# A graph network on one core: the attention row terms through memory, a reordered opening, and a bias added by DMA

## The reference

```python
h = relu(layernorm(x)); skip = x
for l in range(3):
    si, sj = h @ attn_w[l, :d], h @ attn_w[l, d:]
    scores = leaky(si[:, :, None] + sj[:, None, :] + attn_b[l], 0.2)
    attn = softmax(where(adj + eye > 0, scores, -inf))
    a = layernorm(h + einsum('bij,bjd->bid', attn, h), g1[l], beta1[l])
    h = layernorm(a + gelu(a @ W1[l] + b1[l]) @ W2[l] + b2[l], g2[l], beta2[l])
return skip + h
```

## Time and profile before

| what | value |
|---|---|
| median of 3 runs | 2274.11 us (2273.81 to 2275.63) |
| the profiled execution, its own time | 2274.6 us |
| span of its instructions | 2272.8 us |
| mean granted TensorE clock | 0.996 |
| longest waits of PE | DVE s_j 20.9 us (2 times), DVE g_lo 19.5 us (24 times) |
| longest gaps in the trace of PE before slot 1 | 13.1 us before the first transposes, 7.8, 6.6, 5.2 and 5.0 us |

### The profile page before, as it was taken

The page is one execution under the profiler, slowest core; times in us unless marked ns, Lnnn a source line. Parts: engine busy times, 40 slices in busy tenths (PEclk is TensorE's granted clock), DMA queues, the critical chain, the costliest instruction groups (busy, mean ns, idle before and its releaser), DMA issues.

```text
span 2272.8 us, 46153 instructions
## 1 busy us (share of the span) xinstructions
PE 2202.7 (97%) x15456; PEld 1520.7 (67%) x15456; DVE 1869.1 (82%) x5889; ACT 1887.6 (83%) x3496; POOL 1908.4 (84%) x1640
## 2 busy tenths in 40 slices
...
DMA packets 383722, 145.23 MB, mean 64 GB/s; under 512 B 314240, under 2 KB 381824, under 8 KB 383488
## 3 DMA queue, kind: packets, MB, share of 16 engines
...
...
## 4 chain that ended last, share of the span: by engine, by line
PE 79%; DVE 17%; issue 3%; ACT 1%; DMA 1%; POOL 0%; DVEq 0%; SPq 0%
PE p_hid L448 36%; PE p_pair L462 35%; PE p_pair L500 5%; DVE g_lo L682 3%; DVE bn L689 3%; DVE res L765 2%; DVE adj_in L710 2%; DVE dots L727 2%; PE p_pair L486 2%; DVE dots L730 1%; DVE p_lo L777 1%; DVE mv L694 0%; PE p_pair L473 0%; DMA pT_hi<-p_hi 0%; DMA adj_in<-in_adj 0%
## 5 line engine op out<-in xcount | busy, mean ns | idle before, releaser
L462 PE MATMUL p_pair<-w_hi,g_hi 128*128 128x256 f16 x3072 | 839.1, 273 | 0.0
L462 PE MATMUL p_pair<-w_lo,g_hi 128*128 128x256 f16 x3072 | 839.1, 273 | 0.0
L462 PE MATMUL p_pair<-w_hi,g_lo 128*128 128x256 f16 x3072 | 839.0, 273 | 0.0
L556 ACT ACTIVATE p_hid<-p_hid,b_eff 128x512 f32<-128x512 f32 x768 | 503.4, 655 | 293.3 <-PE p_hid L448 291.8
L682 DVE TENSOR_TENSOR g_lo<-p_hid,g_hi 128x512 f16<-128x512 f32 x768 | 518.0, 683 | 44.0 <-ACT g_hi L561 36.1
L448 PE MATMUL p_hid<-hT_hi,w_hi 128*128 128x512 f16 x1536 | 458.2, 380 | 26.0 <-DVE g_lo L682 19.5
L561 ACT ACTIVATE g_hi<-p_hid 128x512 f16<-128x512 f32 x768 | 458.7, 597 | 24.3
L448 PE MATMUL p_hid<-hT_lo,w_hi 128*128 128x512 f16 x1536 | 458.6, 380 | 0.9 <-DMA hT_lo<-h_lo 0.9
L448 PE MATMUL p_hid<-hT_hi,w_lo 128*128 128x512 f16 x1536 | 457.8, 380 | 0.0
L937 POOL TENSOR_TENSOR rstd<-var_eps,minus_half 128x4 f32<-128x4 f32 x224 | 230.5, 1029 | 266.1 <-DVE minus_mean L697 266.1
L462 PEld LDWEIGHTS p_pair<-w_hi,g_hi 128*128 128x128 f16 x3072 | 301.2, 98 | 107.6 <-issue 0.8
...
## 6 DMA issues: line engine op xcount, KB each, us to landing
...
adj_in<-in_adj SPq DMA_DIRECT2D x32, 256.0 KB, 3.3
...
pT_hi<-p_hi SPq DMA_TRANSPOSE x96, 2.4
pT_lo<-p_lo SPq DMA_TRANSPOSE x96, 2.4
hT_hi<-h_hi SPq DMA_TRANSPOSE x96, 3.6
```

The costliest lines, as they stand in the source:

```text
L462: mm = pe.matmul(ff_banks(s)[:, t, :], g[i][:, nodes], w[l][:, c, :], start=(c == 0 and t % 2 == 0 and n == 0), stop=(c == C - 1 and n == ...
L556: act.activation(p_hid[k][:], p_hid[k][:], ACT.Gelu, bias=b1_eff[:, l, c:c + 1], scale=1.0 / WSCALE).then_inc(gelu_ready, 1)
```

## The change

It has four parts.

- **Row terms.** From item 4 on, `spread_sj` is gone from PE. SP writes the 512 numbers s_j (128 nodes by 4 graphs, four bytes each) of item s+4 to a buffer in memory at the head of slot s, and at the end of the slot reads them back as one row broadcast to all partitions, 256 KB, into one SBUF buffer `sj_rows`. `add_scores` reads that buffer.
- **One slot further ahead.** Dot products, input statistics, normalization and input load run one slot earlier than before. The mask stays at s+4.
- **Opening.** The probabilities of items 0 and 1 are transposed by PE into PSUM; ACT copies the high half, DVE subtracts for the low half. Loads, statistics, residuals and deviations are reordered; inputs 4 to 7 of the first round are loaded straight into their feature buffers, masks 4 and 5 are made by POOL in slots 0 and 1. Pieces of the weights of layers 1 and 2 move from slots 0 to 3 to slots 3 to 11, one in each slot and engine; the bias folds move to slots 2 and 7. Slots 0 to 11 are written out, and the loop body is slots 12 to 35.
- **b2** is added to the rows of beta1 by an accumulating DMA of POOL.

The changed lines, with the engine's block above each part; counters and names that only follow from them are left out:

```diff
-FIRST_LOOP_SLOT = 4
+FIRST_LOOP_SLOT = 12
...
-FOLD_AT = {4: 1, 6: 2}
+FOLD_AT = {5: 1, 10: 2}
...
+sj_rows = sb("sj_rows", [P, T, N])
+sj_memory = [nc.dram_tensor(f"sj_memory{i}", [T, N], F32).ap() for i in range(2)]
...
+def pair_half(i, h):
+    return p_pair[i][:, 2 * h:2 * h + 2, :].rearrange("p a (u n) -> p (a u) n", n=N)
 def sj_bank(s):
-    return p_pair[s % 2][:, 0:2, :].rearrange("p a (u n) -> p (a u) n", n=N)
+    return pair_half(1, 1) if s == 2 else pair_half(s % 2, 0)
+def by_memory(r, s):
+    return not (isinstance(r, int) and r == 0 and s < 4)
+def sj_total(r, s):
+    return total(r, s, 16, 16 - 4 * 16)
+def bias_bank(s):
+    return pair_half(s % 2, 0)
+def first_pT(i):
+    return pair_half(0, 1 - i)
...
-act_pieces = dict(zip([(0, 6), (0, 7), (1, 0), (1, 3), (2, 0), (2, 3), (3, 0), (3, 3)], pieces[4:]))
-dve_pieces = dict(zip([(0, 7), (1, 1), (1, 4), (2, 1), (2, 4), (2, 7), (3, 1), (3, 4)], pieces[4:]))
+act_pieces = dict(zip([(3, 0), (4, 3), (5, 3), (6, 3), (7, 3), (8, 3), (9, 3), (10, 3)], pieces[4:]))
+dve_pieces = dict(zip([(s, 0) for s in range(4, 12)], pieces[4:]))
...
 @block.sync
...
+def sj_to_memory(r, s):
+    sp.wait_ge(dots_ready, total(r, s, 8, 8))
+    if later(r, s, 6):
+        sp.wait_ge(sj_in, sj_total(r, s - 2))
+    with nc.allow_non_contiguous_dma("four bytes of each node and graph"):
+        sp.dma_start(sj_memory[s % 2].rearrange("t n -> n t"), s_j[s % RING][:]).then_inc(sj_out, 16)
+def sj_to_rows(r, s):
+    sp.wait_ge(sj_out, sj_total(r, s))
+    if later(r, s, 5):
+        sp.wait_ge(score_steps, total(r, s - 1, 5, 4))
+    sp.dma_start(sj_rows[:].rearrange("p t n -> p (t n)"),
+                 sj_memory[s % 2].rearrange("t n -> (t n)").partition_broadcast(P)).then_inc(sj_in, 16)
 def slot(r, s):
+    first = isinstance(r, int) and (r, s) == (0, 0)
+    if is_item(r, s + 4) and not first:
+sj_to_memory(r, s + 4)
...
-    if is_item(r, s + 4) and layer_of(s + 4) == 0 and group_of(r, s + 4) + 2 < G:
-        sp.wait_ge(x0_ready, group_total(r, s + 4, 4, 4))
-        load_x(group_of(r, s + 4) + 2)
+    if is_item(r, s + 5) and layer_of(s + 5) == 0 and group_of(r, s + 5) + 2 < G:
+        sp.wait_ge(x0_ready, group_total(r, s + 5, 4, 4))
+        load_x(group_of(r, s + 5) + 2)
...
+    if (r, s) == (0, 0):
+        attention_rows(slice(1, L))
+        for dst, v in ((g1_rows, g1), (res_rows, beta1), (g2_rows, g2), (beta2_rows, beta2)):
+            rows_of(dst, v, slice(1, L), more_rows_dma)
...
-        weights(2, s - 1)
+        weights(1, s - 1)
+    if (r, s) in ((0, 5), (0, 7)):
+        weights(2, (s - 5) // 2)
+    if first:
+sj_to_memory(r, s + 4)
+    if is_item(r, s + 4):
+sj_to_rows(r, s + 4)
+def rows_of(dst, v, layers, loaded):
+    sp.dma_start(dst[:, layers].rearrange("p l d -> p (l d)"),
+                 flat(v[layers]).partition_broadcast(P)).then_inc(loaded, 16)
 def next_x(g):
-    if g in (2, 3):
-        sp.wait_ge(x_loaded[g % 2], 16)
-    else:
-        sp.wait_ge(x_loaded[g % 2], 2 * 16)
-        sp.wait_ge(x0_ready, group_total(0, g - 4, 4, 4))
+    sp.wait_ge(x_loaded[g % 2], 16 * (g // 2))
...
 def opening():
+    load_adj(0)
...
-    load_adj(0)
...
-    next_adj(2)
...
+    next_adj(2)
+    columns(b1_col, b1, b1_dma)
+    for dst, v in ((g1_rows, g1), (res_rows, beta1)):
+        rows_of(dst, v, slice(0, 1), rows_dma)
...
-    turn_probs_hi(0, 0)
-    turn_probs_lo(0, 0)
-    for dst, v in ((g1_rows, g1), (b2_rows, b2), (res_rows, beta1)):
-        sp.dma_start(dst[:].rearrange("p l d -> p (l d)"),
-                     flat(v).partition_broadcast(P)).then_inc(rows_dma, 16)
...
-    columns(b1_col, b1, b1_dma)
...
+    next_x(6)
...
-    turn_probs_hi(0, 1)
-    turn_probs_lo(0, 1)
-    weights(1, 0)
-    attention_rows(slice(1, L))
...
-        sp.dma_start(dst[:].rearrange("p l d -> p (l d)"),
-                     flat(v).partition_broadcast(P)).then_inc(rows_dma, 16)
-    weights(1, 1)
+        rows_of(dst, v, slice(0, 1), out_rows_dma)
...
 @block.tensor
...
 def spread_sj(r, s):
-    if later(r, s, 4):
-        pe.wait_ge(res2_ready, total(r, s - 4, 2, 2))
-    if isinstance(r, int) and r == 0 and s in FOLD_AT:
-        fold_bias(FOLD_AT[s], sj_bank(s), 1)
-        pe.wait_ge(bias_ready, FOLD_AT[s] + 1)
...
-    if is_item(r, s + 1) and not (isinstance(r, int) and (r, s) == (0, 0)):
+    if isinstance(r, int) and (r, s) == (0, 2):
...
+    if isinstance(r, int) and r == 0 and s + 1 in FOLD_AT:
+        pe.wait_ge(bias_ready, FOLD_AT[s + 1] + 1)
...
 def slot(r, s):
-        if isinstance(r, int) and r == 0 and (s, c) in ((0, 0), (0, LAG), (3, C - 1)):
-            pe.wait_ge(w_lo_ready, {(0, 0): 2, (0, LAG): 4, (3, C - 1): 4 * L}[s, c])
+        if isinstance(r, int) and r == 0 and (s, c) in ((0, 0), (0, LAG), (7, C - 1), (11, C - 1)):
+            pe.wait_ge(w_lo_ready, {(0, 0): 2, (0, LAG): 4, (7, C - 1): 8, (11, C - 1): 12}[s, c])
...
-        if c == 3 and isinstance(r, int) and r == 0 and s + 3 in FOLD_AT:
+        if c in (3, 4) and isinstance(r, int) and r == 0 and s + 3 in FOLD_AT:
...
-            fold_bias(FOLD_AT[s + 3], sj_bank(s + 3), 0)
-        if c == 4 and is_item(r, s + 3):
-            spread_sj(r, s + 3)
+            fold_bias(FOLD_AT[s + 3], bias_bank(s + 3), c - 3)
+        if isinstance(r, int) and (r, s, c) == (0, 0, 4):
+            spread_sj(0, 3)
...
+            transpose_probs(1)
+        if isinstance(r, int) and (r, s, c) == (0, 0, 1):
+            spread_sj(0, 2)
...
+            pe.wait_ge(bias_ready, 1)
+def transpose_probs(i):
+    pe.wait_ge(probs_ready, 4 * i + 4)
+    for t in range(T):
+        mm = pe.transpose(first_pT(i)[:, t, :], probs[:, t, :], ident[:])
+    mm.then_inc(pT_psum, 1)
 def opening():
+    transpose_probs(0)
+    aggregate(0, 0)
...
-    aggregate(0, 0)
+    fold_bias(0, fold_bank, 1)
...
-    fold_bias(0, fold_bank, 1)
-    spread_sj(0, 2)
-    pe.wait_ge(bias_ready, 1)
...
 @block.scalar
...
-        act.wait_ge(p_lo_ready, total(r, s - 1, 1, 1))
+    if isinstance(r, int) and r == 0 and s in (1, 2):
+        act.wait_ge(pT_psum, s)
+    if later(r, s, 3):
+        act.wait_ge(p_lo_ready, total(r, s - 1, 1, -1))
...
+def copy_probs(i):
+    act.wait_ge(pT_psum, i + 1)
+    if i:
+        act.wait_ge(agg_ready, i)
+    act.activation(pT_hi[:], first_pT(i), ACT.Copy).then_inc(pT_hi_ready, 16)
-        if c == 3 and is_item(r, s + 4) and layer_of(s + 4) == 0:
-            norm_input(r, s + 4)
+        if isinstance(r, int) and (r, s, c) == (0, 0, 1):
+            norm_input(0, 4)
+        if c == 3 and is_item(r, s + 5) and layer_of(s + 5) == 0:
+            norm_input(r, s + 5)
...
-        if isinstance(r, int) and (r, s, c) == (0, 3, 7):
+        if isinstance(r, int) and (r, s, c) == (0, 7, 7):
...
 def opening():
...
-    high_probs(0, 0)
+    copy_probs(0)
...
-    norm_input(0, 2)
...
-    norm_input(0, 3)
+    norm_input(0, 2)
...
+    norm_input(0, 3)
...
-    high_probs(0, 1)
...
+    copy_probs(1)
...
 @block.vector
...
 def add_scores(r, s):
-    dve.wait_ge(sj_rows_ready, total(r, s, 1, 1))
+    if by_memory(r, s):
+        dve.wait_ge(sj_in, sj_total(r, s))
+    else:
+        dve.wait_ge(sj_rows_ready, s + 1)
+    rows = sj_rows if by_memory(r, s) else sj_bank(s)
...
-        dve.scalar_tensor_tensor(out=scores[:, t, :], in0=sj_bank(s)[:, t, :], scalar=s_i[q][:, t:t + 1],
+        dve.scalar_tensor_tensor(out=scores[:, t, :], in0=rows[:, t, :], scalar=s_i[q][:, t:t + 1],
...
+def first_low_probs(i):
+    dve.wait_ge(pT_hi_ready, 16 * i + 16)
+    if i:
+        dve.wait_ge(agg_ready, i)
+    dve.tensor_tensor(pT_lo[:], first_pT(i), pT_hi[:], ALU.subtract).then_inc(pT_lo_ready, 16)
 def slot(r, s):
-    starts = is_item(r, s + 5) and layer_of(s + 5) == 0
+    starts = is_item(r, s + 6) and layer_of(s + 6) == 0 and not (isinstance(r, int) and (r, s) == (0, 0))
...
-            dve.wait_ge(stat_steps[0], group_total(r, s + 5, 10, 4))
+            dve.wait_ge(stat_steps[0], group_total(r, s + 6, 10, 4))
...
-            first_residual(1)
...
+            first_input(5)
...
-            input_statistics(r, s + 5)
+            input_statistics(r, s + 6)
...
-            aggregates(0, group_total(r, s + 5, 10, 8))
+            aggregates(0, group_total(r, s + 6, 10, 8))
...
-            add_bias(FOLD_AT[s + 3], sj_bank(s + 3))
+            add_bias(FOLD_AT[s + 3], bias_bank(s + 3))
...
-        if c == 6 and is_item(r, s + 4):
-            dot_products(r, s + 4, 0)
-            dot_products(r, s + 4, 1)
-        if c == 7 and is_item(r, s + 4) and layer_of(s + 4) == 0:
+        if isinstance(r, int) and (r, s, c) == (0, 0, 4):
+            dot_products(0, 4, 0)
+            dot_products(0, 4, 1)
+        if c == 6 and is_item(r, s + 5):
+            dot_products(r, s + 5, 0)
+            dot_products(r, s + 5, 1)
+        if isinstance(r, int) and (r, s, c) == (0, 0, 7):
+            first_input(6)
+        if isinstance(r, int) and (r, s, c) == (0, 2, 7):
```

(57 more changed lines are left out.)

9 lines of the change are left out of this document (4 added, 5 removed).

## The result

The changed kernel takes **2508.09 us** (median of four runs, 2506.48 to 2510.16) where the kernel before took 2273.96: a ratio of 1.103 (1.101 to 1.104). I had forecast 2229 and a range up to 2250. It is 10% slower. The profiled execution took 2510.2 us, its span 2508.2.

What follows compares the result with a forecast made beforehand. PE's issue was taken to bound ordinary slots (22.59 us), with DVE close behind in crowded ones. Steady gains of 33.1 us (27.7 + 2.3 + 3.1) plus 12.1 for the opening, off 2274.6, gave 2229 us, range 2210 to 2250.

Steps and rivals of the forecast that it cites:

- Row terms, on DVE: Scores' four adds, reading the row from SBUF: 0.5 us more per slot, hidden in ordinary slots, making DVE the crowded slots' bound.
- the rows show lengthening, not blocks: Argument at the scores against DVE waiting for whole POOL instructions: a weight subtraction took 2.28 us beside POOL, 1.28 without.
- Rival 3: Scores wait for whole POOL instructions: DVE takes 25.11 us in 15 crowded slots, 27.9 us more, 2257 in all; chance 0.07.
- ordinary slots hide 2.36 in 3.08: In ordinary slots, DVE's idle 1.18 + 1.90 us would cover a wait for one whole POOL instruction, 2.36 us.
- crowded slots: 15 slots with one item's mask and another's input statistics, bound by DVE: 22.75 + 0.5 = 23.25 us instead of 23.40.
- Row terms, on PE: Four transposes fewer in each of slots 12 to 92: 0.44 us each, ordinary slots 22.59 to 22.15, 27.7 us over 63 slots.
- One slot further ahead: Statistics shift against the mask, so five slots a round carry both instead of six: gains of 2.3 and 3.1 us.
- no contention: Sign to look for: crowded slots at 22.96 us, PE's loop without transposes, if reading the row from SBUF costs DVE nothing.
- Row terms, on SP: Two DMAs and three waits added to SP's queue per slot: both hidden, cost nothing; low transpose issued 6.0 us into the slot.
- Rival 5: On SP, the write of four-byte pieces holds up the probabilities' transposes: slower, 2395 if held 12 us; chance 0.04.
- The opening: Slots 0 to 11: slot 0 starts at 40, slot 1 at 80, slot 12 at 337.7 against 349.83, gaining 12.1 us.
- The sum: Whole kernel: 33.1 us steady plus 12.1 us opening, 45.2 us off the profiled 2274.6, forecast 2229 us.

Runs made afterwards that it cites:

- experiment 1: Changed kernel with the score add's second tensor taken from PSUM in place of the mask, which is left out (computes something else): 2244.02 us, ratio 0.987.
- experiment 3: Changed kernel with ACT copying the row that came through memory from SBUF to PSUM, where DVE's adds read it: 2243.23 us, ratio 0.986.
- experiment 5: Changed kernel with three POOL instructions per slot (product and sum of h_res, difference h_lo) each issued as two halves: 2385.69 us, ratio 1.049.
- experiment 7: Kernel of experiment 3 with the attention and norm row loads of layers 1 and 2 moved to the ends of slots 1 and 2: 2239.40 us, ratio 0.985.
- experiment 8: Kernel of experiment 7 with SP turning h_lo ahead of loading x of a later graph, instead of behind it: 2223.38 us, ratio 0.978.

## Why the prediction was wrong, point by point

**The step that failed** is "Row terms, on DVE": "That is 1.00 us more for 1,024 elements, 0.5 us for the 512 of the four adds." I read the one lengthened row (2.28 against 1.28 us) as a rate and scaled it by elements. It was a wait for an instruction of POOL, and what counts there is how many instructions wait and how long POOL's are. Measured: 7.10 - 1.13 = 5.97 us in an ordinary slot, twelve times my figure. The rows of before could have told me, and "No row shows that form" was wrong. DVE's `p_lo` subtraction reads two SBUF tensors in every slot. By source its 96 instructions take 679 ns at the least (0.68 us at 89.50, where POOL idles) and 1,219 in the median. One of them, and POOL beside it, in the slot of the earlier trace rows:

```profile
834.20 1.22 DVE L777 TENSOR_TENSOR p_lo<-probs,p_hi 128x512 f16<-128x512 f32 x1
```
```profile
833.61 1.27 POOL L981 TENSOR_TENSOR X<-norm,g_rows 128x512 f32<-128x512 f32 x1
834.96 1.60 POOL L988 TENSOR_TENSOR X<-X,beta_rows 128x512 f32<-128x512 f32 x1
```

It ends 0.54 us behind the end of POOL's L981 (834.88), and over 80 of the 96 end 0.54 or 0.55 us behind the end of a POOL instruction: a wait with a length of its own behind it, and no rate. The row that I did use says the same. POOL's timeline beside it (DVE's L675 from 146.92 to 149.20):

```profile
146.67 1.45 POOL L981 TENSOR_TENSOR X<-norm,g_rows 128x512 f32<-128x512 f32 x1
148.20 2.12 POOL L988 TENSOR_TENSOR X<-X,beta_rows 128x512 f32<-128x512 f32 x1
```

A POOL instruction was running until 148.12, and the DVE instruction ended 1.08 us after that, about its own length. It could lose 1.2 us at most because that POOL instruction was a short one of 512 elements and already under way. POOL's next one in turn took 2.12 us, where the same line takes 1.28 to 1.6 elsewhere. Both sides waited, for whole instructions. I wrote "the rows show lengthening, not blocks" from a length alone, without looking at what it ended with.

**Rival 3 had the mechanism and the wrong count.** It is the rule of the Trainium skill ("SBUF — State Buffer", "Who interferes with whom"), to which I gave 0.07 against one row; experiments 1, 3 and 5 agree with it. But I priced one wait of 2.36 per slot, and at that price even this rival came out faster than the kernel before (2257); my 0.04 for slower lay with another rival. Three of four adds wait in an ordinary slot, since POOL starts its next instruction between two of them. So "ordinary slots hide 2.36 in 3.08" was not the test to make; 5.97 against 3.08 leaves 2.9, and the slots are 2.6 us longer than the 22.15 that I forecast (2.1 longer than before). In the crowded slots my own sum, rightly filled, comes out: DVE's work of 22.75 plus 5.5 - 1.13 for the adds, which take about 5.5 us there, is 27.1, and the slot is 26.99.

**Row terms, on PE: right.** 22.15 us wherever the adds don't wait (experiments 1, 3, 7, 8).

**One slot further ahead, and crowded slots.** The bound that I named for "no contention", 22.96, is there in five of the fifteen crowded slots of experiment 8 (22.95 or 22.96), and slots with the mask alone take 22.38, for which I had 22.37. That the fifteen average 23.15, near my 23.25, is no confirmation: the half microsecond of contention that I had put in does not occur there. In experiment 3 they average 23.85, up to 26.17, which is 9 us in all above my figure, from a cause that I had not looked for: h_lo's transpose behind the load of x on SP. SP's order mattered there, not in the place where I costed it.

**Row terms, on SP: right in the steady part, wrong in slot 1.** The low transpose of the probabilities is issued at 911.57, 7.5 us into its slot (I had 6.0), right behind the end of its input `p_lo` (911.55), and PE never waits for it there; the write and the read-back issue in 0.36 and 0.34 us. The write itself I had too short: I put it between 2.4 and 7.6 us, nearer the small end. By the semaphore events of the changed kernel's trace it lands 8.4 to 12.9 us behind its issue, in the 47 slots whose record is complete. The 15.6 us between write and read-back in that slot (909.24 to 924.85) hide it. Rival 5 (the four-byte pieces) did not occur: experiments 1 and 3 make all of those writes and have slots of 22.15. But in slot 1 the read-back follows the write at once, ahead of the transposes, and the write stood behind loads. Moving the loads gave back 5.4 us, and I had gone through SP's list for the steady slots alone.

**The opening: size nearly right by luck.** With the adds mended, slot 12 starts at 338.83 (experiment 3) where I had 337.7. Slot 0 starts at 41.44 (I had 40) and is 35.58 long (I had 40); slot 1 starts at 77.02 (80) but takes 31.15 (22.5); slot 2 takes 25.55 (28.3). Those errors cancel. In the changed kernel itself nothing of this arrived: slots 4 to 11 pay 25.6 us for the adds, against experiment 3. The DMA that adds b2 was rightly costed at nothing: POOL issues it at 36.56 in 1.08 us, and POOL's only wait for a DMA in the whole run is 2.7 us for an adjacency.

**The sum.** From slot 12 to slot 93 experiment 3 takes 1825.4 us, 20.0 less than before, against my 33.1, and its total is 2243, 14 above the forecast. Only with the two further moves of SP's list, which the change does not have, does experiment 8 get to 32.0 less and 2223. So the forecast of 2229 lies between the change with its row in PSUM and that kernel with SP's list mended as well. It is the price of neither, and not of the change as made.
